# Attention over keys: reciprocal of the softmax sums by logarithm, exponential and a Newton step, normalisation on GpSimd, bias matmuls first

## The reference

```python
# fourth sublayer (causal)
q, k, v = split(x @ W_attn + b_attn)
att = einsum('bqhd,bkhd->bhqk', q, k) / sqrt(8) / temperature
att = att + where(causal, slopes[:, None, None] * (pos_k - pos_q), -inf)
y = einsum('bhqk,bkhd->bqhd', softmax(att), v) @ W_proj + b_proj
x = layernorm(x + y)
# fifth sublayer (masked)
scores = einsum('bhqd,bhkd->bhqk', x @ Wq.T, ctx @ Wk.T) / sqrt(8)
p = softmax(where(mask == 0, -1e9, scores))
x = layernorm(x + einsum('bhqk,bhkd->bqhd', p, ctx @ Wv.T) @ Wo.T)
```

## Time and profile before

| | us |
|---|---|
| median of 3 runs | 1576.04 (1575.76 to 1583.57) |
| the profiled execution | 1577.56 |
| its span, as the trace shows it | 1575.6 |

### The profile page before, as it was taken

How to read it: one execution, slowest core, us unless ns; L and a number is a source line. 1 busy time by engine, 2 the same in 40 slices (tenths; PEclk the granted TensorE clock), 3 DMA queues, 4 the chain that set the end, 5 groups by cost and what they waited for, 6 DMA issues and landing times.

```text
span 1575.6 us, 63489 instructions
## 1 busy us (share of the span) xinstructions
PE 1318.1 (84%) x26424; PEld 854.0 (54%) x26438; DVE 1219.3 (77%) x2629; ACT 1057.1 (67%) x2244; POOL 762.1 (48%) x1558
## 2 busy tenths in 40 slices
PE   5888888898876787776677789999999899998897
PEld 2555555565544444444333356666666666666685
DVE  2455666666556888887899879898999999999865
ACT  2565666676656778886667667777777777777655
POOL 2334545455445778777888733333333232332233
PEclk9888899999878889995656789999999999999999
DMA  7000000000000000000000000000000000000012
GB/s 195 14 2 2 3 3 3 2 4 3 2 9 15 17 23 17 24 11 16 1 1 1 1 2 3 3 3 3 2 3 10 23 17 16 17 19 14 2 42 68
DMA packets 28670, 24.27 MB, mean 15 GB/s; under 512 B 3676, under 2 KB 23906, under 8 KB 28386
## 3 DMA queue, kind: packets, MB, share of 16 engines
q1 hardware_dynamic: 28386, 20.21, 4.6%
HBM read 15.94 MB, written 4.19 MB: 13 GB/s over the span
## 4 chain that ended last, share of the span: by engine, by line
PE 31%; issue 24%; POOL 21%; ACT 15%; DVE 8%; SPq 0%; DMA 0%; POOLq 0%; another core or an unknown queue 0%; DVEq 0%; ACTq 0%
PE keys_T L589 7%; ACT keys_pexp L674 5%; POOL gla_low L1155 4%; PE keys_E L485 3%; ACT xs L317 3%; POOL cross_pairs L836 3%; POOL gla_yg L1179 3%; ACT keys_pT L656 2%; PE keys_E L528 2%; POOL cross_spread L803 2%; DVE ffn_hh L1993 2%; PE keys_O L596 2%; POOL gla_sq L1172 2%; PE keys_S L331 1%; ACT keys_vz L647 1%
## 5 line engine op out<-in xcount | busy, mean ns | idle before, releaser
L656 ACT ACTIVATE keys_pT<-keys_T 128x512 f32<-128x512 f32 x256 | 152.4, 595 | 107.5 <-PE keys_T L589 104.2
L340 POOL TENSOR_SCALAR keys_spread<-keys_kT,keys_heads 128x512 f32<-128x512 f32 x128 | 86.7, 696 | 259.2 <-ACT keys_kT L620 259.2
L350 DVE TENSOR_REDUCE keys_mx<-keys_S 128x16 f32<-128x1024 f32 x128 | 156.5, 1223 | 36.9 <-PE keys_S L555 22.0
L589 PE MATMUL keys_T<-ident_sb,keys_pexp 128*128 128x128 f32 x1024 | 165.5, 285 | 22.5 <-ACT keys_pexp L674 18.5
L589 PEld LDWEIGHTS keys_T<-ident_sb,keys_pexp 128*128 128x128 f32 x1024 | 113.1, 141 | 98.4 <-ACT keys_pexp L674 50.4
L353 DVE TENSOR_TENSOR keys_pe_in<-keys_S,keys_mx 128x1024 f32<-128x1024 f32 x128 | 156.7, 1224 | 4.4
L674 ACT ACTIVATE keys_pexp<-keys_pe_in 128x1024 f32<-128x1024 f32 x128 | 134.2, 1048 | 0.2 <-DVE keys_pe_in L353 0.2
L709 DVE RECIPROCAL keys_rinv<-keys_O 128x128 f32<-128x128 f32 x128 | 120.4, 941 | 0.1
L1615 DVE COPY_PREDICATED gla_at<-gla_node,gla_GP 128x256 f32<-128x256 int32 x128 | 64.7, 506 | 68.7 <-ACT gla_at L1469 65.4
L1172 POOL TENSOR_TENSOR gla_sq<-gla_o 128x512 f32<-128x512 f32 x32 | 33.2, 1039 | 141.1 <-ACT gla_o L1477 141.1
L1155 POOL TENSOR_TENSOR gla_low<-gla_ex,gla_kT 128x128 f32<-128x128 f32 x160 | 71.3, 477 | 55.5 <-ACT gla_ex L1460 55.5
(11 more groups left out here) (285 smaller groups left out, 3717.6 us busy)
## 6 DMA issues: line engine op xcount, KB each, us to landing
context<-in_ctx_T SPq DMA_DIRECT2D x32, 256.0 KB, 2.6
xs<-in_x SPq DMA_DIRECT2D x8, 512.0 KB, 7.3
out_x<-xs SPq DMA_DIRECT2D x16, 256.0 KB, 2.3
keys_mask_q<-keys_mask_b SPq DMA_DIRECT2D x64, 1.0 KB
keys_bias_right_f<-in_alibi_right SPq DMA_DIRECT2D x1, 512.0 KB, 4.2
ffn_w<-in_L_ffn_w_gate_T SPq DMA_DIRECT2D x1, 256.0 KB, 4.6
ffn_w<-in_L_ffn_w_up_T SPq DMA_DIRECT2D x1, 256.0 KB, 4.8
ffn_w<-in_L_ffn_w_down_T SPq DMA_DIRECT2D x1, 256.0 KB, 5.5
```

The costliest lines, as they stand in the source:

```text
L340: nc.gpsimd.tensor_scalar(spread[:, :, :, j, :].rearrange("q t s k -> q (t s) k"), flat.rearrange("q (a k) -> q a k", k=SEQ), heads[:, j:j ...
L350: nc.vector.tensor_reduce(m, quads(S), X, ALU.max).then_inc(c["mx"], 1)
L589: last = nc.tensor.transpose(T[:, j * P:(j + 1) * P], pexp[:, t % 2, (4 * half + j) * P:(4 * half + j + 1) * P], sh.ident[:, :])
L656: nc.scalar.activation(pT[:, t % 2, 4 * half:4 * half + 4, :].rearrange("q n k -> q (n k)"), T[:, :], ACT.Copy).then_inc(c["pT"], 1)
```

## The change

- DVE no longer computes `reciprocal` of the sums. ACT takes the logarithm of the sums (`lns`, 128x128 from PSUM) and then the exponential of its negative (`r0`), a first value of the reciprocal. This stands in the new `inverse_sums`, behind `exp(n)` in ACT's slot, for tile n-2.
- DVE refines it by one Newton step in two instructions, `sr` = sums times r0 and `rinv` = (sr - 2) times r0, which is the negative of the reciprocal. Outputs times `rinv` give the negated `oT`; the residual is therefore x minus the projection (`less_residual`) where it was x plus it. `weighted(n-3)` stays first in DVE's slot and now waits for `r0`. `sr` and `rinv` have one buffer, `rinv` had two.
- The normalisation of tile n-7 goes from ACT to POOL, first in POOL's slot.
- In the causal half the four bias matmuls come ahead of the score matmuls.
- ACT loads the table set `natural_log_exp_and_others` once where it loaded `exp_and_others`; the count of table loads in the program stays the same.

```diff
--- before.py
+++ after.py
@@ -397,10 +397,11 @@
         pe_in = sb("pe_in", [P, 2, H * SEQ])
         pexp = sb("pexp", [P, 2, H * SEQ])
         pT = sb("pT", [P, 2, 8, P])
-        rinv = sb("rinv", [P, 2, P])
+        r0 = sb("r0", [P, 2, P])
         oT = sb("oT", [P, 2, P])
         assert nc.sbuf_base <= sh.early_end
         start_at(nc, ctx, "keys", sh.ffn_end)
+        lns, sr, rinv = sb("lns", [P, P]), sb("sr", [P, P]), sb("rinv", [P, P])
         vz = sb("vz", [P, 2, G, 2, 4, 96])
         start_at(nc, ctx, "keys_f", max(nc.sbuf_base, sh.second_end))
         bias_left_f, bias_right_f = sb("bias_left_f", [P, TILE]), sb("bias_right_f", [P, H * SEQ])
@@ -412,7 +413,7 @@
         c = Counts(sh, nc, "keys")
         c.new(*NORM_SEMS, "weights", "zeros", "prep", "bo", "ctx0", "ctx1", "mask0", "mask1", "xr",
               "xT_done", "xT", "k_done", "kT", "q_done", "qT", "spread", "v_done", "v", "scores", "mx", "sub", "exp",
-              "pT_done", "pT", "pv", "rinv", "oT")
+              "pT_done", "pT", "pv", "lns", "r0", "sr", "rinv", "oT")
 
         loads = [(dst[:, :], x[n]) for i, x in enumerate((ac, am))
                  for dst, n in ((wq[i], "wq"), (wk[i], "wk"), (wv[i], "wv"), (wo[i], "wo"))]
@@ -465,11 +466,18 @@
                     nc.gpsimd.tensor_tensor(x, x, bo[:, :].unsqueeze(1).to_broadcast([P, G, D]), ALU.add) \
                         .then_inc(c["xr"], 1)
 
+            def normalise(g, p, t):
+                c.await_nth(pool, "rstd", g, NORM_OPS, NORM_OPS)
+                nc.gpsimd.tensor_scalar(tokens(sh, g, t, 1), b.h[:, p, t, :], b.rstd[:, p, t:t + 1],
+                                        b.nshift[:, p, t:t + 1], ALU.mult, ALU.add).then_inc(c["norm"], 1)
+
             def slot(g, p, t):
+                if n := back(g, p, t, 7, 2 * NG):
+                    normalise(*n)
                 if (n := back(g, p, t, 3, 2 * NG)) and n[2] == G - 1:
                     pool_moments(nc, pool, sh, b, c, n[0], n[1])
 
-            return Part(early, (lambda g, p, t: None, slot), 3, groups=2 * NG, prepare=prepare)
+            return Part(early, (lambda g, p, t: None, slot), 7, groups=2 * NG, prepare=prepare)
 
         @stage.on("tensor")
         def _(pe):
@@ -541,7 +549,12 @@
                     if masked:
                         pe.wait_ge(c[f"mask{p}"], (g - NG - p) * 32 + 64)
                 c.free_last(pe, "sub", g, t, 1)
-                tensor_scores(nc, S, qT[:, p, t * TILE:(t + 1) * TILE], spread[:, p, t, :, :, :], stop=False)
+                if not masked:
+                    for r in range(4):
+                        nc.tensor.matmul(S[:, r * 512:r * 512 + QH * SEQ], bias_left[:, :],
+                                         bias_right[:, r * QH * SEQ:(r + 1) * QH * SEQ], start=True, stop=False)
+                last = tensor_scores(nc, S, qT[:, p, t * TILE:(t + 1) * TILE], spread[:, p, t, :, :, :],
+                                     start=masked, stop=not masked)
                 if masked:
                     for s in range(2):
                         for r in range(4):
@@ -550,10 +563,6 @@
                                 mask_one[32 * r:32 * r + 1, :],
                                 mask_q[32 * r:32 * r + 1, p, t, s, :].unsqueeze(1).to_broadcast([1, QH, SEQ]),
                                 start=False, stop=True)
-                else:
-                    for r in range(4):
-                        last = nc.tensor.matmul(S[:, r * 512:r * 512 + QH * SEQ], bias_left[:, :],
-                                                bias_right[:, r * QH * SEQ:(r + 1) * QH * SEQ], start=False, stop=True)
                 last.then_inc(c["scores"], 1)
 
             def weigh(g, p, t):
@@ -656,6 +665,14 @@
                 nc.scalar.activation(pT[:, t % 2, 4 * half:4 * half + 4, :].rearrange("q n k -> q (n k)"), T[:, :],
                                      ACT.Copy).then_inc(c["pT"], 1)
 
+            def inverse_sums(g, p, t):
+                c.await_tile(act, "pv", g, t)
+                c.free_last(act, "r0", g, t, 1)
+                nc.scalar.activation(lns[:, :], OB[t % 2][:, P:2 * P], ACT.Ln).then_inc(c["lns"], 1)
+                c.await_tile(act, "lns", g, t)
+                c.free_last(act, "oT", g, t, 2)
+                nc.scalar.activation(r0[:, t % 2, :], lns[:, :], ACT.Exp, scale=-1.0).then_inc(c["r0"], 1)
+
             def first(g, p, t):
                 if n := back(g, p, t, 1, 2 * NG):
                     take(*n, 0)
@@ -663,17 +680,17 @@
             def second(g, p, t):
                 if n := back(g, p, t, 1, 2 * NG):
                     take(*n, 1)
-                if n := back(g, p, t, 7, 2 * NG):
-                    scalar_normalise(nc, act, sh, b, c, *n)
                 if n := back(g, p, t, 0, 2 * NG):
                     gg, _, tt = n
                     if gg == 0 and tt == 0:
-                        nc.scalar.preload_act_table_set("exp_and_others")
+                        nc.scalar.preload_act_table_set("natural_log_exp_and_others")
                     c.await_tile(act, "sub", gg, tt)
                     c.free_last(act, "pT_done", 2 * gg, 2 * tt + 1, 4)
                     nc.scalar.activation(pexp[:, tt % 2, :], pe_in[:, tt % 2, :], ACT.Exp).then_inc(c["exp"], 1)
-
-            return Part(early, (first, second), 7, groups=2 * NG)
+                if n := back(g, p, t, 2, 2 * NG):
+                    inverse_sums(*n)
+
+            return Part(early, (first, second), 2, groups=2 * NG)
 
         @stage.on("vector")
         def _(dve):
@@ -702,14 +719,28 @@
                         .then_inc(c["prep"], 1)
             R0 = 2
 
+            def less_residual(g, p, t):
+                c.await_tile(dve, "out_done", g, t)
+                c.free_tile(dve, "norm", g, t)
+                nc.vector.tensor_tensor(b.h[:, p, t, :], tokens(sh, g, t, 1), OB[t % 2][:, 2 * P:2 * P + D], ALU.subtract) \
+                    .then_inc(c["h"], 1)
+                c.await_tile(dve, "h", g, t)
+                if t == 0:
+                    c.free_group(dve, "rstd", g, NORM_OPS)
+                nc.vector.bn_stats(b.stats[:, p, t, :], b.h[:, p, t, :]).then_inc(c["stats"], 1)
+
             def weighted(g, p, t):
                 o = OB[t % 2]
                 c.await_tile(dve, "pv", g, t)
-                c.free_last(dve, "oT", g, t, 2)
-                nc.vector.reciprocal(rinv[:, t % 2, :], o[:, P:2 * P]).then_inc(c["rinv"], 1)
+                c.await_tile(dve, "r0", g, t)
+                nc.vector.tensor_tensor(sr[:, :], o[:, P:2 * P], r0[:, t % 2, :], ALU.mult).then_inc(c["sr"], 1)
+                c.await_tile(dve, "sr", g, t)
+                c.free_last(dve, "oT", g, t, 1)
+                nc.vector.scalar_tensor_tensor(rinv[:, :], sr[:, :], 2.0, r0[:, t % 2, :], ALU.subtract, ALU.mult) \
+                    .then_inc(c["rinv"], 1)
                 dve.wait_ge(c["rinv"], g * G + (t + 1 + R0))
                 c.free_last(dve, "out_done", g, t, 2)
-                nc.vector.tensor_tensor(oT[:, t % 2, :], o[:, 0:P], rinv[:, t % 2, :], ALU.mult).then_inc(c["oT"], 1)
+                nc.vector.tensor_tensor(oT[:, t % 2, :], o[:, 0:P], rinv[:, :], ALU.mult).then_inc(c["oT"], 1)
 
             def slot(g, p, t):
                 if n := back(g, p, t, 3, 2 * NG):
@@ -720,7 +751,7 @@
                     gg, p2, tt = n
                     if tt == 0 and gg < NG:
                         c.await_nth(dve, "xr", gg, 1, 1)
-                    vector_residual(nc, dve, sh, b, c, gg, p2, tt, OB[tt % 2][:, 2 * P:2 * P + D])
+                    less_residual(gg, p2, tt)
 
             return Part(lambda g, p, part: None, (lambda g, p, t: None, slot), 3, groups=2 * NG, prepare=prepare)
 
```

## The result

| | before | changed |
|---|---|---|
| median of the runs, us | 1578.3 | 1690.0 |
| ratio to before, with interval | | 1.0746 [1.071, 1.0782] |
| span of the profiled execution, us | 1575.6 | 1688.2 |
| first to last maximum of the stage, us | 914.0 to 1484.2: 570.2 | 901.3 to 1588.6: 687.3 |
| last maximum to the end, us | 91.4 | 99.6 |

The change costs 112 us. The forecast was 92 us, 1668 us in all with a range from 1632 to 1706. The direction and the mechanism came as forecast; the size was 20 us too small.

What follows compares the result with a forecast made beforehand. It took the added DVE-ACT wait ring, 4.96 us per slot, with longer v and causal k slots, as the bound. Causal 45.4 plus masked 46.4 made 91.8 us more, 1668 us; 80% range 1632 to 1706.

Steps and rivals of the forecast that it cites:

- What bounds: Step following the queue behind DVE's added wait: max(n) can start only after a trip to ACT and back.
- the wait that the forecast named first: DVE idle ahead of `sr`, ended by ACT's `r0`, in nearly every slot, about 1.1 us of it.
- The ring of 4.96: Every slot: maximum, subtraction, exponential, logarithm, `r0`, `sr`, `rinv`, `oT`, next maximum in series; 4.96 us, against 4.52 and 4.45.
- PE's path: Second path between exponentials, through PE's scores, transposes and ACT's copies; causal v slot 5.94 us, k slot 5.06.
- The k slot: Causal k slot: 5.06 us by the path through PE; masked k slot: 4.96 us.
- The q slot: Causal q slot taken like k, less k's surplus of 0.10: 4.96 us; masked q slot also 4.96.
- The masked v slot: Exponential through `oT` to `output` 2.57, to second transposes 1.40, their copy 1.34, next activation 0.50: 5.81 us.
- The wait does not bind, 1547 us: Rival: `r0` comes in time, so DVE has room and the gain at the exponential stands; 1547 us, chance 5%.
- Every slot only the ring, 1637: Rival: PE's path in v slots is shorter than read, so a group is 4 x 4.96 = 19.84; 1637 us, chance 12%.
- Clock: Rival: new instructions dear, or PE's clock falls in the less busy stage (42 us); priced at 1700 us, chance 23%.
- Normalisation in the new ring: Moving it off ACT, worth up to 0.38 us a slot before, gains nothing where ACT waits for `sub`.
- Bias first: Causal bias matmuls ahead of scores: taken as nothing, bounded at 0.1 either way in three slots a group, 5 us.

Runs made afterwards that it cites:

- e2_ring: Kernel before plus only a wait: DVE's old reciprocal of tile n-3 also waits for exp(n-1); 1701.6 us, ratio 1.0778.
- e8_older: Kernel before plus only a wait: DVE's old reciprocal of tile n-3 also waits for exp(n-2); 1581.3 us, ratio 1.0031.
- e1_early: Changed kernel with ACT's logarithm and r0 of tile n-2 moved to the first half of its slot, one exponential sooner; 1554.5 us, ratio 0.9845.
- e6_recip: Changed kernel with normalisation back on ACT ahead of the exponential and bias matmuls last again, leaving only the new reciprocal; 1728.7 us, ratio 1.0969.
- e13_early: Second measurement of the same program as e1_early, against the kernel before; 1542.5 us, ratio 0.9788.
- e3_norm: Kernel before with only the normalisation moved from ACT to GpSimd (POOL); 1553.7 us, ratio 0.9844.
- e9_norm_bias: Kernel before with normalisation on GpSimd and causal bias matmuls ahead of the scores, old reciprocal kept; 1544.5 us, ratio 0.9802.

## Why the prediction was right, and where its size was off

**What bounds.** The first step, following the queue behind the added wait rather than the busy time, was right. `e2_ring` and `e8_older` show that the wait's tile alone decides, and `e1_early` that without it the change gains. The profile's waits of the changed kernel, over the stage, have the wait that the forecast named first:

```profile
DVE keys_sr L736 <- ACT keys_r L674: 184.8, 126, 2.8
```

126 of 128 tiles wait. The mean of the idle time named there is 1.47 us, where the forecast had "about 1.1" in nearly every slot: it is 1.18 in the x slots, 1.2 to 1.35 in the k and q slots, and 2.13 in the v slots, where the exponential comes latest. Another sign failed: ACT was to wait for `sub` ahead of the exponential in three of four slots. It did so in one, the x slot, for 0.32 us; elsewhere its own copies ended no earlier than `sub`.

**The ring of 4.96 is 5.04.** Step by step: maximum to subtraction 1.25 (1.26 forecast), subtraction to exponential 1.26 (1.26), exponential to logarithm 0.96 (0.96), logarithm to `r0` 0.29 (0.30), **`r0` to `sr` 0.41 (0.31)**, `sr` to `rinv` 0.33 (0.33), `rinv` to `oT` 0.33 (0.33), `oT` to maximum 0.21 (0.21). Seven of eight terms hold to 0.01. The mis-sized one is made of an exponential that takes 0.31 us and not the 0.27 of the copy in the earlier trace rows, and of 0.10 from ACT to a waiting DVE, where I took the 0.04 of the ring's other hand-overs. The ring is 0.08 longer for it, and it reaches six of the eight slots of two groups (not the causal k and v slots, where PE's path is longer), 0.08 to 0.10 in each: 16 x 0.55 = 9 of the 24 us by which the forecast of the stage fell short.

The Trainium skill, "ScalarE: Activation LUTs", section "What ACT_TABLE_LOAD costs", gives one formula for any function, which makes an estimate of 0.29 us for 128 elements. The trace has 0.26 to 0.28 for the logarithm from PSUM and 0.31 for the exponential in SBUF: the sum agrees to 0.01, each single one does not.

**The slots.** The four of a causal group, forecast and measured: x 4.96 and 5.05, k 5.06 and 5.38, q 4.96 and 5.20, v 5.94 and 6.00. Masked: k 4.96 and 5.30, x 4.96 and 5.05, q 4.96 and 5.14, v 5.81 and 6.00. The causal group is 0.71 longer and the masked one 0.79, and 16 x (0.71 + 0.79) = 24 us. Beside the ring's 9 us, three terms make it.

*The k slot, rinv at 0.56.* Once in a group this instruction takes nearly twice its time. The changed kernel's timeline of DVE and of POOL there:

```profile
1129.01 0.29 DVE L736 TENSOR_TENSOR keys_sr<-keys_O,keys_r 128x128 f32<-128x128 f32 x1 [1.26 <-ACT keys_r L674]
1129.33 0.56 DVE L739 SCALAR_TENSOR_TENSOR keys_rinv<-keys_sr,keys_r 128x128 f32<-128x128 f32 x1
...
1130.14 1.21 DVE L350 TENSOR_REDUCE keys_mx<-keys_S 128x16 f32<-128x1024 f32 x1
```

```profile
1127.06 2.70 POOL L340 TENSOR_SCALAR keys_spread<-keys_kT,keys_heads 128x512 f32<-128x512 f32 x4 [9.61 <-ACT keys_kT L629]
```

The long ones are 30 of 128, nearly one in each of the 32 groups, and all 30 start beside a spread of the keys that has 0.42 us to go and end 0.13 to 0.14 us behind it. Here the fourth spread ends at 1129.76 and `rinv` at 1129.89. I had bounded `rinv` between 0.25 and 0.41 from its own duration alone; that GpSimd's spread, which is in the kernel before too, could hold it up was not in the sum. The moved normalisation is not what does it: `e6_recip` has none on GpSimd, and yet one long `rinv`, beside the spread in the same way (rows in the last section). I had meant to decide this by whether the long ones vanish there. All but that one do, but since the exponential stands 0.38 us later behind the normalisation, `rinv` meets only the last 0.06 us of the spread. In the last group, which has no early work and so no spread, the k slot takes 5.03. The full 0.27 lies in the k slot: 5.11 by PE's path (exponential 1122.23 to exponential 1127.34, forecast 5.06) and 0.27 give the 5.38; 5.04 and 0.27 the masked 5.30. That is 32 x 0.27 = 9 us, as much as the ring's term.

*The q slot.* I took PE's path to be that of a k slot. It leads through `oT` instead, like that of a masked v slot. The timeline of PE, a masked q and the v slot behind it:

```profile
1410.46 0.49 PE L605 MATMUL keys_O<-keys_wo_masked,keys_oT 128*128 128x128 f32 x2 [0.23 <-DVE keys_oT L743]
1410.78 1.02 PE L493 MATMUL keys_E<-keys_xT,keys_wq_masked 128*128 128x512 f32 x2
...
1415.57 0.49 PE L605 MATMUL keys_O<-keys_wo_masked,keys_oT 128*128 128x128 f32 x2 [0.31 <-DVE keys_oT L743]
1415.99 1.15 PE L536 MATMUL keys_E<-keys_wv_masked,context 128*64 128x64 f32 x32
1417.07 0.66 PE L598 MATMUL keys_T<-ident_sb,keys_pexp 128*128 128x128 f32 x4
```

and ACT behind it:

```profile
1407.79 1.06 ACT L689 ACTIVATE keys_pexp<-keys_pe_in 128x1024 f32<-128x1024 f32 x1 [0.32 <-DVE keys_pe_in L353]
...
1412.91 1.06 ACT L689 ACTIVATE keys_pexp<-keys_pe_in 128x1024 f32<-128x1024 f32 x1
...
1418.91 1.05 ACT L689 ACTIVATE keys_pexp<-keys_pe_in 128x1024 f32<-128x1024 f32 x1
```

From the exponential to `output` is 2.67, and from there to the next exponential 2.45 in the q slot (1410.46 to 1412.91), together 5.12 (1407.79 to 1412.91); ACT does not wait for the subtraction there, its copies come last. In the causal half the biased copy of the queries takes 0.78 and not 0.69, and the slot is 5.20. Forecast was 4.96 for both; beyond the ring's 0.10 that is 0.14 and 0.08 a slot, 16 x 0.22 = 4 us.

*The masked v slot.* By the forecast's steps: exponential to `output` 2.66 (2.57), `output` to the second transposes 1.50 (1.40), 1.34 and 0.50 as forecast, in sum 6.00 (5.81). The first is the 0.10 of the ring. The second stands at the `output` itself: behind a wait, PE's next matmul starts 0.42 us after it, where it started 0.32 after the `output` of the earlier trace rows, which did not wait: 16 x 0.10 = 2 us. The 0.05 and 0.06 of PE's paths in the causal k and v slots add 2 more, and 9 + 9 + 4 + 2 + 2 is 26 of rounded terms for the 24.

**What the stage does not hold.** The measured span has three pieces: 117 us more from the first maximum to the last, 8 us more from there to the end, and 13 us less ahead of the stage, 112.6 in all. The 8 us are PE's clock behind the stage. A window of the changed kernel, and then one of before at about the like place:

```profile
1610.00:1620.00 10.00, 10.00 (x46) 8.01 (x46) 5.26 (x28) 2.94 (x9) 2.04 (x5) 0.50 0.00 1
```

```profile
1510.00:1520.00 10.00, 10.00 (x85) 8.28 (x82) 7.65 (x37) 7.54 (x21) 3.60 (x10) 1.00 0.20 54
```

At 0.50 PE is at 1.2 GHz throughout, busy all the time, and gets through 46 instructions in 10 us where before had 85 at 1.00. (Before was at 0.78 in the 10 us ahead of that window.) `e1_early` has 0.50 to 0.57 there for 30 us and `e13_early`, the same program, 0.91 to 1.00, and their pieces behind the last maximum are 100.0 and 89.3 us. So this piece belongs to the execution and not to the change. The same holds for the 13 us ahead of the stage, in code that no kernel here touches: the stage begins at 901.3 us in the changed kernel, 914.0 in before, and at 918.7 in `e1_early` and 905.4 in `e13_early`, one program. That the two pieces nearly cancel is luck. The forecast of the whole fell short by 20 us: 25 in the stage (24 in the groups and 1 in its first and last slots), less the 5 that the two pieces leave.

**The rivals.** *The wait does not bind, 1547 us.* It was named with the condition that the exponential ahead of `r0(n-3)` belong to a tile before n-1. `e1_early` is that kernel, and `e13_early` its second measurement: 1554.5 and 1542.5. The price was near, and its condition was the right one. *Every slot only the ring, 1637.* The q and v slots show PE's and ACT's path; it did not hold. *Clock.* In the stage the grants stayed at 1.00 and 0.98 though PE's busy share fell to 84% and 79% (the 0.98 comes from the last 20 us, with 0.74; up to 1570 us it is 1.00), so my 42 us, scaled from one stretch with 0.92, were not to be had from busy shares. `e6_recip` shows that the danger is real, in a kernel next to this one.

**The other parts.** Normalisation in the new ring "worth nothing": true in the x slot, and the 0.38 in q and v slots was in the sum, as the difference of `e6_recip` shows. Alone it is worth 24 us (`e3_norm`), of which the ring lets the 0.38 of the q and v slots show. GpSimd takes 0.45 us for one, in the forecast at most 0.70, and its cover held. Bias first: nothing in the ring, 0.10 in PE-bound slots, at the gaining end of the bound given.

## What to carry to other kernels

Before a wait is added to an in-order engine, write down which tile's work stands ahead of the awaited instruction on the other engine, and whether that work needs what is queued behind the wait. If it does, the slot is the sum of the whole ring, whatever the busy times say; here a wait for one tile older cost nothing. Work that is moved off an engine is only a gain if that engine is the last to be waited for, and a busy share does not tell: DVE was busy for 97% of the masked half in `e9_norm_bias`, and PE, with 95%, set the pace.
